# Who subtracts the softmax minimum, and who makes the low half of attention's output: one graph-attention and mixture-of-experts kernel on one core

## What is computed

```python
q, k, v = (split_heads(layernorm(x) @ W + b) for W, b in ...)
scores = einsum('bhqd,bhkd->bhqk', q, k) / sqrt(16)
scores = where(adj > 0, scores, -9e15)
out = einsum('bhqk,bhkd->bhqd', softmax(scores), v)
x = x + out.reshape(b, n, 128) @ Wo + bo
...
x = x + shared_ffn(layernorm(x)) + routed_ffn(layernorm(x))
```

## Time and profile before

| what | value |
|---|---|
| median of 3 runs | 1289.5 us (1286.26 to 1293.18) |
| profiled execution, its own time | 1284.22 us |
| its span | 1282.2 us |
| granted TensorE clock over the span | 0.94 |
| busy over the span: PE, DVE, ACT, POOL | 83%, 79%, 70%, 67% |
| busy between 250 and 300 us, of 50: PE, DVE, ACT, POOL | 45.92, 43.94, 45.38, 41.48 us, clock 1.00 |

### The profile page before, as it was taken

How to read it: one execution, slowest core, us unless ns; L and a number is a source line. 1 busy time by engine, 2 the same in 40 slices (tenths; PEclk the granted TensorE clock), 3 DMA queues, 4 the chain that set the end, 5 groups by cost and what they waited for, 6 DMA issues and landing times. The chain is left out here.

```text
span 1282.2 us, 40036 instructions
## 1 busy us (share of the span) xinstructions
PE 1061.0 (83%) x12584; PEld 765.9 (60%) x12585; DVE 1007.3 (79%) x2443; ACT 900.2 (70%) x1962; POOL 862.9 (67%) x894
## 2 busy tenths in 40 slices
PE   4899999999999999962789998899999999889100
PEld 2666666666666666641466776577777777778100
DVE  6688888888888888864577887677877777667498
ACT  3999999999999999950667886666666666567000
POOL 4267888888888888757667776277777777766200
PEclk9999999999999999995889999899999999999655
DMA  3355444444444443333346552544444444333398
GB/s 89 59 98 108 102 98 107 115 107 114 112 111 112 102 97 98 83 71 99 95 114 172 150 145 69 86 98 100 101 99 94 99 99 98 75 68 73 135 357 302
DMA packets 306212, 144.64 MB, mean 113 GB/s; under 512 B 224807, under 2 KB 284365, under 8 KB 306139
## 3 DMA queue, kind: packets, MB, share of 16 engines
q1 hardware_dynamic: 271738, 101.31, 34.7%
q0 software_dynamic: 16896, 33.86, 8.1%
q10 hardware_dynamic: 17504, 8.59, 2.3%
HBM read 47.95 MB, written 54.04 MB: 80 GB/s over the span
## 5 line engine op out<-in xcount | busy, mean ns | idle before, releaser
L1463 POOL DMA_INDIRECT pairs_dram<-x_rows x272 | 279.1, 1026 | 124.1 <-issue 80.9
L1141 ACT ACTIVATE hid<-Z,biases 128x512 f32<-128x512 f32 (+1 forms) x336 | 207.9, 631 | 139.7 <-PE Z L1109 101.4
L1156 DVE SCALAR_TENSOR_TENSOR h<-hid,h 128x512 f16<-128x512 f32 (+1 forms) x288 | 183.7, 650 | 54.4 <-ACT h L1132 49.5
L1121 PEld LDWEIGHTS Y<-w,h 128*128 128x128 f16 x3168 | 185.5, 99 | 27.5 <-issue 9.9
L1121 PE MATMUL Y<-w,h 128*128 (+1 forms) x3168 | 192.6, 220 | 11.0 <-DVE h L1156 9.5
L524 DVE TENSOR_REDUCE smin<-S 128x8 f32<-128x1024 f32 x128 | 156.6, 1223 | 25.5 <-PE S L818 25.2
L1254 POOL DMA_INDIRECT slots_dram<-x_rows,pair_slot x128 | 131.8, 1030 | 47.7 <-issue 24.2
L684 ACT ACTIVATE probs<-S,smin 128x128 f32<-128x128 f32 x512 | 147.9, 387 | 21.2 <-DVE smin L524 18.1
L1109 PE MATMUL Z<-x_rows,w 128*128 128x512 f16 (+1 forms) x720 | 150.1, 355 | 10.4 <-DMA x_rows<-slots_dram 5.9
L352 POOL DMA_INDIRECT slots_dram<-x_rows,pair_slot x116 | 118.5, 1022 | 31.6 <-issue 23.0
L1132 ACT ACTIVATE h<-hid 128x512 f16<-128x512 f32 (+1 forms) x176 | 105.8, 601 | 20.8 <-ACT hid L1141 5.5
(11 more groups left out here) (222 smaller groups left out, 2163.4 us busy)
## 6 DMA issues: line engine op xcount, KB each, us to landing
y_pairs<-pairs_dram SPq DMA_DIRECT2D x32, 512.0 KB, 6.0
x_res<-in_x_dram SPq DMA_DIRECT2D x32, 256.0 KB, 3.4
adj<-in_adj_dram SPq DMA_DIRECT2D x32, 256.0 KB, 3.2
xT_dram<-xT SPq DMA_DIRECT2D x32, 256.0 KB, 3.7
xTu<-xT_dram SPq DMA_DIRECT2D x32, 256.0 KB, 3.4
out_dram<-x_res ACTq DMA_DIRECT2D x16, 512.0 KB, 10.7
pairs_dram<-x_rows POOLq DMA_INDIRECT x272
slots_dram<-x_rows,pair_slot POOLq DMA_INDIRECT x256, 2.3
```

Of the source, the lines that this page charges most:

```text
L1121: mm = pe.matmul(self.Y[:, b % 2, j], self.piece(b)[:, k, c, j * P:(j + 1) * P], self.w2[:, m, :, c][:, e, :], start=c == 0 and n == 0, st ...
L1141: act.activation(self.hid[:, c, 0:w], self.bank(b, c)[:, 0:w], ACT.Gelu, bias=bias[:, c:c + 1], scale=1.0 / (XS * WS)).then_inc(self.gelu_ ...
L1156: dve.scalar_tensor_tensor(out=self.piece(b)[:, 1, c, 0:w], in0=self.hid[:, c, 0:w], scalar=HS, in1=self.piece(b)[:, 0, c, 0:w], op0=ALU.m ...
L1463: pool.indirect_dma_start(pairs_dram, bass.IndirectOffsetOnAxis(ap=pair_of[n][:, j:j + 1], axis=0), y_sb[n % NY][:, j], None, bounds_check ...
```

## The change

Four heads of eight subtracted by DVE in every step become six, four, four, six for j = 0, 1, 2, 3, so that ACT exponentiates two heads straight from S in j = 0 and 3, and six in its later instruction. `low_output` leaves DVE's j = 3 and becomes an instruction of POOL, inside `split`, between its second multiplication and its copy; for group 0 it stands alone in POOL's turn for g = 1.

```diff
-SHIFTED = 4
+SHIFTED = (6, 4, 4, 6)
...
+        def low_output(g):
+
+            wait(pool, "ahi_done", g + 1)
+            pool.tensor_tensor(at16[:, :, 1], attn[:, :, :, :].rearrange("p j h c -> p j (h c)"), at16[:, :, 0],
+                              ALU.subtract).then_inc(s["asplit_done"], 1)
+
-        def split(g):
+        def split(g, between=None):
...
             pool.tensor_tensor(xc2[:], xc2[:], rs2s[:].unsqueeze(2).to_broadcast([P, GT, P]),
                                ALU.mult).then_inc(s["xs2_done"], 1)
+            if between is not None:
+                low_output(between)
             set_up(pool, g)
...
+            if g == 1:
+                low_output(0)
             if has(g, 2):
-                split(g - 2)
+                split(g - 2, g - 1 if g < NG else None)
...
-        def softmax_shift(t, b):
+        def softmax_shift(t, b, n):
...
-            dve.tensor_tensor(probs[:, b, 0:SHIFTED].rearrange("p (r e) k -> p r e k", e=2),
-                              smin[:, 0:SHIFTED].rearrange("p (r e) -> p r e", e=2).unsqueeze(3).to_broadcast([P, SHIFTED // 2, 2, P]),
-                              S_heads[:, 0:SHIFTED // 2], ALU.subtract).then_inc(s["sub_done"], 1)
+            dve.tensor_tensor(probs[:, b, 0:n].rearrange("p (r e) k -> p r e k", e=2),
+                              smin[:, 0:n].rearrange("p (r e) -> p r e", e=2).unsqueeze(3).to_broadcast([P, n // 2, 2, P]),
+                              S_heads[:, 0:n // 2], ALU.subtract).then_inc(s["sub_done"], 1)
...
-                    softmax_shift(t, j % 2)
+                    softmax_shift(t, j % 2, SHIFTED[j])
...
-                if j == 3 and has(g, 1):
-                    low_output(g - 1)
...
-                    for h in range(SHIFTED, H):
+                    for h in range(SHIFTED[j], H):
...
-                    pr = probs[:, j % 2, 0:SHIFTED]
+                    pr = probs[:, j % 2, 0:SHIFTED[j]]
                     act.activation(pr, pr, ACT.Exp).then_inc(s["exp_done"], 1)
```

More of the change, by code:

```diff
@@ L478, in residual @@
                                      in1=xg, op0=ALU.mult, op1=ALU.add).then_inc(s["x2_done"], 1)
[L480 to L484, removed]
         def stats2(g):
```

## The result

The changed kernel takes 1313.15 us, the median of 4 runs (1312.28 to 1317.13), against 1289.94 for 4 runs of the kernel before on the same chip: a ratio of 1.0187 with a 95% interval of 1.0152 to 1.0221. It is slower, by 1.5 to 2.2%. The profiled execution took 1312.28, 28.06 more than that of before; its span is 1310.5, with a granted clock of 0.938 beside 0.94.

A forecast was written before the change was run, and what follows sets the result against it. Attention was taken as bound by a 16.99 us ring through several engines. 26 × (0.27 + 0.82) = 28.3, plus 1 for groups 2 and 3, on 1284.2 gave 1313.5 profiled, 1318.5 as median; range 1295 to 1323.

The forecast's parts named there:

- The ring: Attention's cycle from DVE's minimum of j = 2 through ACT, PE, DVE, POOL and `choose` to the next: 16.99 us.
- The sign named for a wrong base: The forecast's base is wrong if the minimum of j = 1 does not move later against that of j = 0.
- Six heads in j = 0, +0.27: DVE's longer subtraction in j = 0, where DVE has no gap, adds 0.27 us per group; bounds 0 and 0.27.
- Six heads in j = 3: the mask loses: DVE's mask, 0.27 later, starts 0.04 to 0.05 behind POOL's second `split` multiplication, waits, and takes about 1.3, not 0.42.
- The price of a lost mask: A mask held behind POOL's multiplication moves PE's scores of j = 0 from 290.36 to 291.18: +0.82 us per group.
- the 0.4 between the mask's end and the scores: Before the change, DVE's mask was read as done 0.4 us before PE's scores of j = 0 need it.
- The mask loses in every group: DVE's mask, starting second to POOL's multiplication, was taken to be held up in all groups; chance 0.52.
- The "alternates" rival: DVE's mask is held up in one of the loop's two groups, not the other: 18.1 us, 1307.6; chance 0.15.
- `place` behind six heads, +0.03: DVE's `place`, 0.27 later, delays PE's product with V by 0 to 0.05 us; 0.03 taken.
- the first rival: DVE's mask slips in before POOL's multiplication, leaving 0.27 + 0.03 per group: 7.8 us, 1297.3; chance 0.17.
- The low part, 0: Moving `low_output` to POOL costs 0: its 1.17 plus 0.08 gap hides in POOL's 1.33 us wait for statistics.
- the step that carried over 5.3 from the runs of before: The runs' median, 1289.5, lay 5.3 above the profiled execution; that was added to 1313.5, giving 1318.5.

The follow-up runs named there:

- e9: Kernel before, with only DVE's statistics in j = 0 moved ahead of its normalisation of ON: 1280.70 us beside 1291.50, ratio 0.9936.
- e2: Changed kernel with six heads in j = 0 only (6,4,4,4), low part on POOL: 1288.93 us beside 1285.45 for before, ratio 1.0039.
- e3: Changed kernel with six heads in j = 3 only (4,4,4,6), low part on POOL: 1311.18 us, ratio 1.0206 to before.
- e6: Changed kernel with each mask made one group earlier: 1292.3 us beside 1286.07 for before, ratio 1.0053.
- e5: Changed kernel with PE's wait for the mask put last ahead of the scores of j = 0: 1312.19 us, ratio 1.0206 to before.
- e1: Changed kernel with four heads in every step, low part still on POOL: 1288.13 us beside 1285.45 for before, ratio 1.0014.
- e7: Changed kernel with four heads throughout, masks one group ahead and j = 0 statistics before normalising: 1280.34 us beside 1286.07 for before, ratio 0.9958.
- e4: Kernel before with heads 6,4,4,6, low part left on DVE: 1316.09 us, ratio 1.0242 to before.
- e10: Whole change with masks one group ahead and j = 0 statistics before normalising: 1285.49 us beside 1291.50 for before, ratio 0.9945.

## Why the prediction was right, and where it was off

**The bound.** The ring was read rightly, but for the mask, which in every second group already held PE's scores before the change. What moved on it came out at every station: the minimum, the statistics, POOL's line 318 and the compare, which still ends 0.04 to 0.05 behind POOL. That the compare is held by POOL was only inferred from two rows; e9 shows it, since the compare falls to 0.19 once the two no longer meet. The sign named for a wrong base did not appear: the minimum of j = 1 comes 4.12 behind that of j = 0 in the changed kernel (311.38 less 307.26), 3.86 before.

**Six heads in j = 0, +0.27.** Right: e2's period grows by 0.24.

**Six heads in j = 3: the mask loses.** Right in kind: e3 shows that it comes from this part alone, e6 that the wait for the mask is nearly the whole price. Two of its numbers were off.

- *The price of a lost mask*, put at 0.82 by the 0.10 of rows 7. That row stood outside the loop. In the loop the scores follow by 0.34 to 0.35, and e5 shows that the waits behind the mask's make the difference. The row of 307.33 above had it in the kernel before. So the 0.4 between the mask's end and the scores, which the prediction read as a lead, was nearly all PE's delay: in every second group the mask had no time to spare at all. A lost group cost 1.37 on average, not 0.27 + 0.82 = 1.09.
- *The mask loses in every group.* It lost in 17 of 24, with starts 0.022 to 0.055 behind; with 0.014 to 0.022 it got through. The distances 0.04 and 0.05 were right for some groups and 0.02 too large for others. The rule cited from the Trainium skill (SBUF — State Buffer, "Who interferes with whom"), that who issues first holds the ports for the whole instruction, agrees with every pair that was clearly apart; by recorded starts it fails up to 0.021, where DVE started second and still went first. Whether DVE had also issued second there, no row shows. The "alternates" rival was nearer in the count and not in the manner: no fixed pattern of groups won.

**`place` behind six heads, +0.03.** Too small: in every steady group of the change the product with V starts 1.32 behind V's projection, where it was 1.22, and 0.15 after `place`'s product. So `place` holds it up by 0.10. But that is not all that a group with a won mask lost. Such a group cost 0.50 on average, not the 0.27 + 0.03 = 0.30 of the first rival: even a short mask now ended later than the product allowed, and the scores came 0.35 after its end, which in the group of 268.55 is 0.94 behind the product instead of 0.84. In e5, with the wait for the mask last, the two groups with a won mask cost 0.33 each. In a lost group the mask covers all this.

**The low part, 0.** Right, by e1 to within 0.3%. Its place in POOL's row was right too: 1.16 alone, where the sum had 1.17. Beside a lost mask it takes 1.34, which was not foreseen and which POOL's wait of 1.87 covers.

**The sum.** For the steady groups 17 × 1.37 + 7 × 0.50 = 26.8 (26.7 before rounding) in place of 24 × 1.09 = 26.2. With 3.7 from the groups before them, 30.3 had gathered at the last mask of attention; less the 2.0 behind it, the span grew by 28.3, and the prediction had 29.3. So the profiled time, 1312.28 against 1313.5, was met partly by luck: a larger price met fewer losses. The median, 1313.15 against 1318.5, was missed by the step that carried over 5.3 from the runs of before (1313.5 and 5.3 make 1318.8; the 1318.5 is a slip). The profiled execution of before lay below all four of its runs, that of the changed kernel only 0.9 below its median. The loss between the medians is 23.2, and between the two profiled executions 28.06.

**Not shown.** Why the distance between mask and multiplication falls on one side of 0.022 in one group and on the other in the next was not tried. Nor was it tried what the mask made ahead gives the kernel before by itself; in e7, where it is made ahead with four heads, the scores come 0.57 behind the product with V in every second group, where the kernel before has 0.82.

## What to carry to other kernels

Where two engines hold each other up for whole instructions, the order of two starts a few hundredths of a microsecond apart can be worth most of a microsecond (1.37 for a lost group, 0.50 for a won one): before moving work on either engine, list the pairs in which they meet, which one leads and by how much, and who waits for the loser. The two cures were cheap: make the loser early enough that nobody waits for it (e6), or reorder one engine's independent work so that the pair no longer meets (e9, 0.64% shorter than the kernel before, with nothing of the change). And take the delay behind a wait from a row of the same loop, with the same waits behind it.

## What the runs showed of the hardware

- Between DVE's mask and POOL's multiplication the order changes at 0.022 to 0.024 by recorded starts: in the change, e4, e5 and e6 every mask up to 0.021 behind won and every one from 0.024 lost; at 0.022 to 0.023 four won and three lost.
- The end of the one that goes second hangs on the end of the first, however far apart they began. Wherever in the twelve traces a mask is lost, it ends 0.28 after the multiplication (0.279 to 0.285; begun 0.02 to 0.05 behind it takes 1.27 to 1.30, begun 0.07 to 0.11 behind, in e10, 1.21 to 1.25). A multiplication that meets a won mask ends 0.89 to 0.90 after the mask, which makes 1.33 instead of 1.04 when they start together.
- Two waits already fulfilled, with values worked out in the loop, cost PE 0.2 between the awaited mask and the scores (0.34 to 0.35 against 0.15 in e5).
